# A decoder layer on one core: the state-space loop's end-of-chunk scaling, moved from VectorE to ScalarE

## The chip, the cores and the metric

The kernel runs on one core of a Trainium2 chip. The metric is the device time of one execution, in microseconds (us). A core has TensorE (matrix products, into PSUM), VectorE, ScalarE, GpSimd (called POOL in the profile) and SyncE (SP), whose queue issues the DMAs. Each engine works through its own instructions in order, and they wait for one another by semaphores.

## The reference, cut to what matters

The layer takes 1024 tokens of width 128 and a context of 6404 rows. It runs a bidirectional state-space block (mamba2), then cross attention to the context with 8 heads, then a mixture of 8 experts. The change lies in the state-space block, which the reference computes for each direction (forward on one half of the width, backward on the other) as a scan over the tokens:

```python
dA = jnp.exp(dt * A)
dtx = dt[..., None] * xh

def step(h, inp):
    dA_t, dtx_t, B_t, C_t = inp
    h = dA_t[:, :, None, None] * h + jnp.einsum('bhp,bn->bhpn', dtx_t, B_t)
    return (h, jnp.einsum('bhpn,bn->bhp', h, C_t))
...
y = jnp.moveaxis(ys, 0, 1) + xh * D[None, None, :, None]
y = y.reshape(b, l, D_INNER) * jax.nn.silu(z)
y = _rmsnorm(y, gnorm_w)
return y @ outp_w.T
```

There are 2 heads of 64 in a direction, and the state has 128 rows.

## The kernel before

The scan is computed in `TC` = 8 chunks of 128 tokens, both directions (`q` = 0, 1) side by side, so that most tiles are 128 x 256: two directions of two heads of 64 columns. Chunk c needs, in this order:

- **`decay_rows`** and **`turned_rows`** (TensorE, for chunk c + 1 inside chunk c): rows of decays into the bank `DECAY`, and the convolved inputs `xc` and `Bc` transposed into the bank `TURNED_XB`.
- **`decays`** (VectorE, L1391): four scans that make the decay matrix `LT`. **`mixing`** (VectorE, L1417): `LT` times the product of B and C (`gram`) gives `Mt`.
- **`inputs`** (VectorE): L1405 makes `Xp`, the inputs times their step dt; L1409 makes `Xw`, that is `Xp` times the decay from each token to the chunk's end, `dcy[:, 1]`. Both are one instruction of 128 x 256. The last chunk needs no `Xw`.
- **`state_rows`** (ScalarE, L989): copies the transposed B out of PSUM as `Bm`.
- In `chunk_pe` (TensorE): the product of C with the old state `Hp` (`ys_ps`); then, behind the waits for `bm_done` and `xw_done`, the product of `Bm` and `Xw` (`s_ps`), which is what the chunk adds to the state; then `turn_gate` of the chunk before, `decay_rows` and `turned_rows` of the next; then the inside product of `Mt` and `Xp` (`yi_ps`); then, in the first `BESIDE` = 4 chunks, two convolutions of the second half of the tokens with `project_out` of the chunk before and `gram` of the next between them.
- **`chunk_act`** (ScalarE): four scaled copies (L1009) of the product with the old state into `t1`; `gate_turned` (L995); `state_rows` of the next chunk; the silu of the first convolution; in some chunks a cast of the context (`high_ctx`, L982); `gate_out` (L1001); the silu of the second convolution (L973 or L976); then, behind `yg_done`, two squares with a sum (L1035) of the gated output.
- **`state`** (VectorE, L1428): four instructions update `Hp`. **`gated`** (VectorE, L1441 and L1444): `t1` plus the inside product, times silu(z), gives `yg`.

VectorE's order in a chunk is `mixing`, `state`, `decays` of the next chunk, `gated`, `inputs` of the next chunk, and then a piece of other work: in chunk 0 the means, variances and inverse roots of the first half of the context, in chunks 1 and 2 statistics of the second half (L1332), in chunk 3 its aggregation (L1357) and roots, and small pieces later. The roots release GpSimd, which scales the context rows. The order on every engine is written out by hand. The convolutions of the second half share PSUM bank 7, so each waits for the silu of the one before:

```python
if n == 7:
    pe.wait_ge(silu_done, 1)
elif n == 8:
    pe.wait_ge(silu_done, 7)
elif n > 8:
    pe.wait_ge(silu_done, n)
```

`Bm` and `Xw` lie in two buffers each, taken in turn by c % 2, in `m_arena`; `Xp`, `t1`, `yg` and `Hp` lie in `w_arena`. When the last chunk's `yg` is there, SP starts the transposing DMAs of the context, and VectorE adds the block's outputs to the residual (L1513), norms the rows and so prepares the queries. Then TensorE finds the row maxima and runs the attention, which takes most of the time, and the experts.

Of the kernel before, what the change touches and what calls it, by code (L numbers as in the profile page):

```python
# [21 lines left out]
ACT, ALU, AX = mybir.ActivationFunctionType, mybir.AluOpType, mybir.AxisListType  # L22
# [4 lines left out]
TC = T // P  # L27
# [3 lines left out]
HD = 64  # L31
# [187 lines left out]
def layer(nc, a, out):  # L219
    ctx = ExitStack()  # L220
    with ctx:  # L221
# [97 lines left out]
        Xp = take([2, 2, P])  # L319
# [16 lines left out]
        dtc, dcy = take([6, 2, TC, 2]), take([3, 2, TC, 2])  # L336
# [13 lines left out]
        Bm, Xw = take([2, 2, P]), take([2, 2, P])  # L350
# [61 lines left out]
        da_ps, xb_ps, g_ps, s_ps, ys_ps, yi_ps = (sem(n) for n in ("da_ps", "xb_ps", "g_ps", "s_ps", "ys_ps", "yi_ps"))  # L412
        gt_ps, gt_sb, out_ps, out_evac = (sem(n) for n in ("gt_ps", "gt_sb", "out_ps", "out_evac"))
        lt_done, xp_done, xw_done, m_done, h_done = (sem(n) for n in ("lt_done", "xp_done", "xw_done", "m_done", "h_done"))
# [510 lines left out]
        def _(act):  # L925
            s = nc.scalar
# [31 lines left out]
            for q in range(2):  # L958
                s.activation(Wout[:, q], PS[:, 7, (1 + q) * P:(2 + q) * P], ACT.Copy,
                             scale=V["gw_" + "fb"[q]]).then_inc(op_sb, 1)  # L960
# [6 lines left out]
            def silu_conv(n):  # L967

                (q, r), half = CONV[n % 8], n // 8
                act.wait_ge(conv_ps, n + 1)  # L970
                if r < 3:
                    dst, bias = (xc, Bc, Cc)[r][:, q, half * QB:(half + 1) * QB], cbias[:, q, r:r + 1]
                    s.activation(dst, PS[:, conv_bank(n), :], ACT.Silu, bias=bias, scale=1 / (XS * WS)).then_inc(silu_done, 1)  # L973
                else:
                    dst = (zs_f, zs_b)[q][:, 4 * half:4 * half + 4, :].rearrange("p c n -> p (c n)")
                    s.activation(dst, PS[:, conv_bank(n), :], ACT.Silu, scale=1 / (XS * WS)).then_inc(silu_done, 1)  # L976
# [7 lines left out]
            def state_rows(c):  # L984
# [3 lines left out]
                    act.wait_ge(s_ps, c - 1)  # L988
                s.copy(Bm[:, c % 2], halves_of(TURNED_XB, 1)).then_inc(bm_done, 1)  # L989

            def gate_turned(c):

                act.wait_ge(gt_ps, c + 1)
                after(act, out_ps, c)
                s.copy(ygT, halves_of(GATE)).then_inc(gt_sb, 1)  # L995
# [7 lines left out]
            def chunk_act(c):  # L1003

                act.wait_ge(ys_ps, c + 1)
                after(act, y2_done, c)
                for q in range(2):
                    for h in range(2):
                        last = s.activation(t1[:, q, h * HD:(h + 1) * HD],  # L1009
                                            PS[:, FROM_STATE, q * P + h * HD:q * P + (h + 1) * HD], ACT.Copy,  # L1010
                                            scale=dcy[:, 0, q, c, h:h + 1])
                last.then_inc(t1_done, 1)
                if c:
                    gate_turned(c - 1)
                if c + 2 < TC:
                    state_rows(c + 1)
                if c < BESIDE:
                    silu_conv(8 + 2 * c)
                if c == TC - 1:
                    root(2)  # L1020
                if 2 <= c < NSOON - 1:
                    high_ctx(c - 2)
                elif c == NSOON - 1:
                    s.activation(rt[:, 5, 0:1], iota8[:, 0:1], ACT.Sqrt)
                elif c == NSOON:
                    high_ctx(c - 3)
                if c:
                    gate_out(c - 1)
                if c < BESIDE:
                    silu_conv(9 + 2 * c)  # L1030
                act.wait_ge(yg_done, c + 1)
                for q in range(2):
                    if c or q:
                        act.wait_ge(sq_done, 2 * c + q)
                    s.activation(sq, yg[:, c % 2, q], ACT.Square, accum_out=ssy[:, q, c:c + 1]).then_inc(sq_done, 1)  # L1035

            for n in range(6):
                silu_conv(n)
            state_rows(0)
            for n in range(6, 8):  # L1040
                silu_conv(n)
            for c in range(TC):
                chunk_act(c)
            gate_turned(TC - 1)
# [212 lines left out]
        def _(dve):  # L1257
            v = nc.vector
# [29 lines left out]
            for c in range(TC):  # L1288
                last = v.bn_stats(stx[:, c, :], x_sb[:, c, :])
# [105 lines left out]
            def inputs(c):  # L1395

                dve.wait_ge(xb_ps, c + 1)
                if c + 1 < TC:
                    dve.wait_ge(bm_done, c + 1)
                if c >= 2:  # L1400
                    dve.wait_ge(yi_ps, c - 1)
                    dve.wait_ge(s_ps, c - 1)
                by_head = lambda x: x.rearrange("p q (h d) -> p q h d", h=2)
                wide = lambda x: x.unsqueeze(3).to_broadcast([P, 2, 2, HD])
                v.tensor_tensor(by_head(Xp[:, c % 2]), by_head(halves_of(TURNED_XB)), wide(dtc[:, 3, :, c, :]),  # L1405
                                ALU.mult).then_inc(xp_done, 1)
                dve.wait_ge(xp_done, c + 1)
                if c + 1 < TC:
                    v.tensor_tensor(by_head(Xw[:, c % 2]), by_head(Xp[:, c % 2]), wide(dcy[:, 1, :, c, :]),  # L1409
                                    ALU.mult).then_inc(xw_done, 1)  # L1410

            def mixing(c):

# [1389 lines left out]
```

## Time and profile before

| | |
|---|---|
| median of 3 runs | 1702.06 us (1701.68 to 1702.9) |
| the profiled execution's own time | 1701.74 us |
| its span in the profile | 1699.7 us |
| mean granted TensorE clock | 0.993 of full speed |
| TensorE busy | 1655.4 us, 97% |
| VectorE busy | 1323.0 us, 78% |
| ScalarE busy | 1069.0 us, 63% |
| GpSimd busy | 873.6 us, 51% |

The times of the views count from the start of the span. Busy time is that of the instructions alone. A row of the timeline gives the start, the time from the start of its first instruction to the end of its last, the engine, the line of the kernel, the operation, what is written from what, and in brackets how long the engine was idle ahead of it and which engine's work ended that. PE is TensorE, DVE VectorE, ACT ScalarE, SPq the queue of SP. The timeline puts like instructions that follow one another in one row ("x4"); next ones may start before the last one's end, as they are pipelined.

### The profile page before, as it was taken

To read this page: it belongs to the slowest core of one execution; us is meant where nothing else is said; L and a number is where in the kernel's file an instruction comes from. 1 tells how busy PE (TensorE), PEld (TensorE's weight loads), DVE (VectorE), ACT (ScalarE), POOL (GpSimd) and SP (SyncE) were. 2 spreads that over 40 slices of the span, in tenths; PEclk is the share of its full clock that TensorE was granted. 3 is DMA by queue.
4 is the path that set the end of the run, shared out by engine and by line. 5 is a ranking of instruction groups with operands and counts; after the bars stand their busy time and mean duration, and the time that the engine had idled before them with its cause. 6 is when DMAs were issued, how large, how long until landed. Compare 5 with 4: busy or idle time off the path is not lost. (4 is left out here: it accounts for less than half of the span.)

```text
span 1699.7 us, 31706 instructions
## 1 busy us (share of the span) xinstructions
PE 1655.4 (97%) x9115; PEld 846.5 (50%) x9115; DVE 1323.0 (78%) x2315; ACT 1069.0 (63%) x1310; POOL 873.6 (51%) x723
## 2 busy tenths in 40 slices
PE   6889999999999999999999999999999999999997
PEld 5754444444444444445454444445454545444496
DVE  7988989877777777777777777777777777776687
ACT  5545665666666666666566666666666666667674
POOL 4767992055454545454545545454545454452365
PEclk9989999999999999999999999999999999999998
DMA  5032110000000000000000000000000000000262
GB/s 186 2 61 73 56 42 0 1 1 1 1 0 0 0 0 0 0 0 0 0 0 1 0 1 0 1 0 1 0 0 0 1 0 1 1 0 1 77 213 77
DMA packets 41058, 34.06 MB, mean 20 GB/s; under 512 B 20447, under 2 KB 35299, under 8 KB 40598
## 3 DMA queue, kind: packets, MB, share of 16 engines
q1 hardware_dynamic: 39862, 30.70, 6.2%
q0 software_dynamic: 1120, 2.31, 0.4%
q8 instruction: 52, 0.85, 0.2%
q14 instruction: 24, 0.20, 0.0%
HBM read 15.27 MB, written 4.23 MB: 11 GB/s over the span
## 5 line engine op out<-in xcount | busy, mean ns | idle before, releaser
L851 POOL TENSOR_TENSOR p_arena<-p_arena 128x512 f16<-128x512 f32 x364 | 596.3, 1638 | 670.8 <-ACT p_arena L1131 670.8
L1122 ACT ACTIVATE p_arena<-PS 128x1024 f16<-128x1024 f32 (+1 forms) x480 | 484.8, 1010 | 508.0 <-PE PS L2032 508.0
L2032 PE MATMUL PS<-a_arena,z_arena 128*128 128x512 f16 (+1 forms) x2832 | 746.5, 380 | 1.4 <-DVE a_arena L1894 1.4
L1578 DVE TENSOR_REDUCE mxs<-PS 128x512 f32 (+1 forms) x900 | 599.7, 672 | 184.5 <-PE PS L2032 180.1
L2032 PE MATMUL PS<-p_arena,z_arena 128*128 128x512 f16 x2800 | 740.2, 379 | 0.4 <-ACT p_arena L1140 0.4
L1131 ACT ACTIVATE p_arena<-PS 128x1024 f32<-128x1024 f32 (+1 forms) x480 | 481.6, 1003 | 0.0
L1610 DVE TENSOR_TENSOR p_arena<-p_arena 128x512 f16<-128x512 f32 (+1 forms) x480 | 395.5, 824 | 85.9 <-ACT p_arena L1131 79.9
L2032 PEld LDWEIGHTS PS<-a_arena,z_arena 128*128 (+1 forms) x2832 | 274.4, 98 | 325.6 <-issue 1.9
L2032 PEld LDWEIGHTS PS<-p_arena,z_arena 128*128 128x128 f16 (+1 forms) x2800 | 271.6, 98 | 313.3 <-ACT p_arena L1140 0.9
L2032 PE MATMUL PS<-z_arena,a_arena 128*128 (+3 forms) x1024 | 352.7, 359 | 3.6 <-DVE mxs L1578 1.9
L2032 PEld LDWEIGHTS PS<-z_arena,a_arena 128*128 128x128 f16 (+1 forms) x1024 | 97.7, 98 | 126.2 <-issue 6.2
L844 POOL TENSOR_TENSOR w_arena<-w_arena 128x256 f16<-128x256 f32 (+1 forms) x50 | 42.1, 842 | 4.2
L781 POOL TENSOR_SCALAR p_arena<-p_arena,mv,rs 128x127 f32<-128x127 f32 x50 | 41.8, 853 | 0.0
L840 POOL TENSOR_SCALAR w_arena<-w_arena 128x256 f32<-128x256 f32 (+1 forms) x50 | 41.4, 828 | 0.0
L2032 PE MATMUL PS<-w_arena 128*128 128x512 f16 (+5 forms) x268 | 35.7, 271 | 3.0 <-DVE w_arena L1326 2.6
L906 POOL TENSOR_TENSOR p_arena<-z_arena,p_arena 128x512 f16<-128x512 f32 x22 | 25.6, 1162 | 25.0 <-ACT p_arena L1217 24.7
L1879 DVE TENSOR_REDUCE mxs<-PS 128x2 f32<-128x1024 f32 (+1 forms) x30 | 33.6, 1184 | 3.4 <-PE PS L2032 3.0
L1608 DVE TENSOR_TENSOR p_arena<-p_arena 4x512 f16<-4x512 f32 x16 | 10.9, 682 | 31.8 <-ACT p_arena L1131 31.8
L2032 PEld LDWEIGHTS PS<-VO,p_arena 128*128 128x128 f32 x256 | 33.4, 191 | 4.3
L897 POOL DMA_INDIRECT xg_dram<-ah_arena,r_arena x14 | 15.0, 1070 | 37.8 <-DVE ah_arena L1751 33.9
L2032 PE MATMUL PS<-z_arena,w_arena 128*128 128x128 f16 x504 | 33.3, 219 | 0.8 <-DVE z_arena L1923 0.3
L2032 PE MATMUL PS<-VO,p_arena 128*128 128x130 f32 (+1 forms) x256 | 33.7, 275 | 0.0
(339 smaller groups left out, 984.7 us busy)
## 6 DMA issues: line engine op xcount, KB each, us to landing
w_arena<-w_arena SPq DMA_DIRECT2D x26, 256.0 KB
w_arena<-in_L_ffn_gate_up_w SPq DMA_DIRECT2D x8, 512.0 KB
p_arena<-w_arena SPq DMA_DIRECT2D x26, 128.0 KB
p_arena<-in_ctx SPq DMA_DIRECT2D x2, 1600.0 KB
w_arena<-in_L_ffn_down_w SPq DMA_DIRECT2D x8, 256.0 KB
a_arena<-in_L_xattn_Wkv SPq DMA_DIRECT2D x1, 1024.0 KB, 7.1
a_arena<-xg_dram SPq DMA_DIRECT2D x12, 65.0 KB, 2.1
xg_dram<-VO SPq DMA_DIRECT2D x1, 715.0 KB, 7.1
```

Source lines behind the costliest of these rows:

```text
L781: g.tensor_scalar(ctx_sb[:, c, 1:P], ctx_sb[:, c, 1:P], mv[:, c, 0:1], rs[:, 3, c:c + 1], ALU.subtract, ALU.mult).then_inc(z_scaled, 1)
L840: g.tensor_scalar(src, src, WS, 0.0, ALU.mult, ALU.add).then_inc(w_scaled, 1)
L844: g.tensor_tensor(lo, src, hi, ALU.subtract).then_inc(stage_used, 1)
L851: g.tensor_tensor(Plo[:, r % 3, QB:2 * QB], P32[:, r % 2, QB:2 * QB], Phi[:, r % 3, QB:2 * QB], ALU.subtract).then_inc(pl_ready, 1)
L897: g.indirect_dma_start(xg_dram, bass.IndirectOffsetOnAxis(ap=posu[:, k, t:t + 1], axis=0), xrow_f[:, k, t, :], None).then_inc(sent, 16)
L906: g.tensor_tensor(lo, hid[:, u % RING], hi, ALU.subtract).then_inc(f_lo, 1)
L1122: s.activation(Phi[:, r % 3, 0:w], ps, ACT.Exp, scale=1 / SSC).then_inc(hi_ready, 1)
L1131: s.activation(P32[:, r % 2, 0:w], ps, ACT.Exp, scale=1 / SSC).then_inc(p32_ready, 1)
L1578: v.tensor_reduce(mxs[:, i, bass.ds(kb, 1)], PS[:, 6 + par, 0:w], AX.X, ALU.max).then_inc(mx_read, 1)
L1610: v.tensor_tensor(Plo[:, r % 3, at:w], P32[:, r % 2, at:w], Phi[:, r % 3, at:w], ALU.subtract).then_inc(lo_ready, 1)
L1879: v.tensor_reduce(mxs[:, i:i + 2, kb:kb + 1], PS[:, pair % 2 * 2:pair % 2 * 2 + 2, 0:w], AX.X, ALU.max).then_inc(mx_read, 2)
L2032: return t.matmul(o, l, r, start=start, stop=stop)
```

## The change

VectorE no longer makes `Xw`: L1409 and the wait ahead of it go. In its place ScalarE gets a function `state_inputs(c)` with four scaled copies of 128 x 64, one for each direction and head, because the scale of an activation is one column. `state_inputs(0)` stands behind the last silu of the first half and ahead of the first chunk; `state_inputs(c + 1)`, for chunks 1 to 6, stands at the end of `chunk_act(c)`, behind the two squares. TensorE still waits for `xw_done` ahead of the state product, and `Xw` keeps its two buffers.

```diff
@@ -988,6 +988,17 @@
                     act.wait_ge(s_ps, c - 1)
                 s.copy(Bm[:, c % 2], halves_of(TURNED_XB, 1)).then_inc(bm_done, 1)
 
+            def state_inputs(c):
+
+                act.wait_ge(xp_done, c + 1)
+                if c >= 2:
+                    act.wait_ge(s_ps, c - 1)
+                for q in range(2):
+                    for h in range(2):
+                        cols = slice(h * HD, (h + 1) * HD)
+                        last = s.activation(Xw[:, c % 2, q, cols], Xp[:, c % 2, q, cols], ACT.Copy, scale=dcy[:, 1, q, c, h:h + 1])
+                last.then_inc(xw_done, 1)
+
             def gate_turned(c):
 
                 act.wait_ge(gt_ps, c + 1)
@@ -1033,12 +1044,15 @@
                     if c or q:
                         act.wait_ge(sq_done, 2 * c + q)
                     s.activation(sq, yg[:, c % 2, q], ACT.Square, accum_out=ssy[:, q, c:c + 1]).then_inc(sq_done, 1)
+                if c + 2 < TC:
+                    state_inputs(c + 1)
 
             for n in range(6):
                 silu_conv(n)
             state_rows(0)
             for n in range(6, 8):
                 silu_conv(n)
+            state_inputs(0)
             for c in range(TC):
                 chunk_act(c)
             gate_turned(TC - 1)
@@ -1404,10 +1418,6 @@
                 wide = lambda x: x.unsqueeze(3).to_broadcast([P, 2, 2, HD])
                 v.tensor_tensor(by_head(Xp[:, c % 2]), by_head(halves_of(TURNED_XB)), wide(dtc[:, 3, :, c, :]),
                                 ALU.mult).then_inc(xp_done, 1)
-                dve.wait_ge(xp_done, c + 1)
-                if c + 1 < TC:
-                    v.tensor_tensor(by_head(Xw[:, c % 2]), by_head(Xp[:, c % 2]), wide(dcy[:, 1, :, c, :]),
-                                    ALU.mult).then_inc(xw_done, 1)
 
             def mixing(c):
 
```

ScalarE's order from the silu of the second convolution of chunk 1 to the first instructions of chunk 2, before (`m_arena` holds `Bm` and `Xw`, and `ssy` the sums of the squares):

```order
L973 ACTIVATE z_arena<-PS,vecs 128x512 [waits conv_ps]
L1035 ACTIVATE w_arena,ssy<-w_arena 128x128 [waits sq_done,yg_done]
L1035 ACTIVATE w_arena,ssy<-w_arena 128x128 [waits sq_done]
L1009 ACTIVATE w_arena<-PS,wt_arena 128x64 [waits y2_done,ys_ps]
L1009 ACTIVATE w_arena<-PS,wt_arena 128x64 x3
L995 COPY w_arena<-PS 128x256 [waits out_ps,gt_ps]
```

and the same place with the change (its lines are numbered 11 higher from `gate_turned` on, and L1046 and L1020 are the squares and the copies into `t1`):

```order
L973 ACTIVATE z_arena<-PS,vecs 128x512 [waits conv_ps]
L1046 ACTIVATE w_arena,ssy<-w_arena 128x128 [waits sq_done,yg_done]
L1046 ACTIVATE w_arena,ssy<-w_arena 128x128 [waits sq_done]
L999 ACTIVATE m_arena<-w_arena,wt_arena 128x64 [waits s_ps,xp_done]
L999 ACTIVATE m_arena<-w_arena,wt_arena 128x64 x3
L1020 ACTIVATE w_arena<-PS,wt_arena 128x64 [waits y2_done,ys_ps]
```

The four copies L999 now stand between the squares of one chunk and `t1` of the next, behind the silu L973.

VectorE's order from the gated output of chunk 3 to the aggregation of the context's second half, before:

```order
L1441 TENSOR_TENSOR w_arena<-w_arena,PS 128x256 [waits gt_ps,sq_done,t1_done,yi_ps]
L1444 TENSOR_TENSOR w_arena<-w_arena,z_arena 128x128 [waits y2_done]
L1444 TENSOR_TENSOR w_arena<-w_arena,a_arena 128x128
L1405 TENSOR_TENSOR w_arena<-PS,wt_arena 128x256 [waits yi_ps,s_ps,bm_done,xb_ps]
L1409 TENSOR_TENSOR m_arena<-w_arena,wt_arena 128x256 [waits xp_done]
L1357 BN_AGGR mv<-st 128x2 x25
```

and with the change (L1451, L1454, L1419 and L1371 are the same statements):

```order
L1451 TENSOR_TENSOR w_arena<-w_arena,PS 128x256 [waits gt_ps,sq_done,t1_done,yi_ps]
L1454 TENSOR_TENSOR w_arena<-w_arena,z_arena 128x128 [waits y2_done]
L1454 TENSOR_TENSOR w_arena<-w_arena,a_arena 128x128
L1419 TENSOR_TENSOR w_arena<-PS,wt_arena 128x256 [waits yi_ps,s_ps,bm_done,xb_ps]
L1371 BN_AGGR mv<-st 128x2 x25
```

The product into `m_arena` and its wait are gone, and the aggregation follows `Xp` at once.

## Rows read from the trace of the kernel before

**Rows 1.** The page, part 1: busy us, share of the span, instructions.
```profile
PE 1655.4 (97%) x9115; PEld 846.5 (50%) x9115; DVE 1323.0 (78%) x2315; ACT 1069.0 (63%) x1310; POOL 873.6 (51%) x723
```

**Rows 2.** Timeline of ScalarE, 36 to 88 us: last silu, squares, copies.
```profile
37.36 0.60 ACT L976 ACTIVATE a_arena<-PS 128x512 f32<-128x512 f32 x1 [0.35 <-PE PS L2032]
...
45.19 0.30 ACT L1035 ACTIVATE w_arena<-w_arena 128x128 f32<-128x128 f32 x1
...
45.92 0.91 ACT L1009 ACTIVATE w_arena<-PS,wt_arena 128x64 f32<-128x64 f32 x4
...
53.79 0.30 ACT L1035 ACTIVATE w_arena<-w_arena 128x128 f32<-128x128 f32 x1
...
61.29 0.30 ACT L1035 ACTIVATE w_arena<-w_arena 128x128 f32<-128x128 f32 x1
...
68.83 0.30 ACT L1035 ACTIVATE w_arena<-w_arena 128x128 f32<-128x128 f32 x1
...
75.90 0.31 ACT L1035 ACTIVATE w_arena<-w_arena 128x128 f32<-128x128 f32 x1 [0.40 <-DVE w_arena L1444]
...
87.15 0.31 ACT L1035 ACTIVATE w_arena<-w_arena 128x128 f32<-128x128 f32 x1 [0.21 <-DVE w_arena L1444]
```

**Rows 3.** Timeline of TensorE: state products (from m_arena) and three inside products.
```profile
37.80 0.61 PE L2032 MATMUL PS<-m_arena 128*128 128x128 f32 x4
...
44.85 0.61 PE L2032 MATMUL PS<-m_arena 128*128 128x128 f32 x4
...
48.07 0.49 PE L2032 MATMUL PS<-w_arena,z_arena 128*128 128x128 f32 x2 [0.83 <-DVE w_arena L1417]
...
53.45 0.61 PE L2032 MATMUL PS<-m_arena 128*128 128x128 f32 x4
...
55.67 0.39 PE L2032 MATMUL PS<-w_arena,z_arena 128*128 128x128 f32 x2
...
61.99 0.61 PE L2032 MATMUL PS<-m_arena 128*128 128x128 f32 x4
...
69.54 0.61 PE L2032 MATMUL PS<-m_arena 128*128 128x128 f32 x4
...
73.03 0.49 PE L2032 MATMUL PS<-w_arena,z_arena 128*128 128x128 f32 x2 [1.11 <-DVE w_arena L1417]
...
76.80 0.68 PE L2032 MATMUL PS<-m_arena 128*128 128x128 f32 x4 [0.82 <-DVE m_arena L1409]
...
82.51 0.68 PE L2032 MATMUL PS<-m_arena 128*128 128x128 f32 x4 [0.56 <-DVE m_arena L1409]
```

**Rows 4.** Timeline of VectorE: the removed product, what follows it, a late mixing.
```profile
67.13 0.42 DVE L1409 TENSOR_TENSOR m_arena<-w_arena,wt_arena 128x256 f32<-128x256 f32 x1
...
67.47 1.75 DVE L1357 BATCH_NORM_AGGREGATE mv<-st 128x2 f32<-128x6 f32 x25
...
72.29 0.69 DVE L1417 TENSOR_TENSOR w_arena<-w_arena,PS 128x512 f32<-128x512 f32 x1
```

**Rows 5.** Behind the loop: SP's first transposes, granted clock, TensorE products at either clock.
```profile
91.93 10.98 SPq L642 DMA_TRANSPOSE z_arena<-z_arena  x3
...
core 0: us, PE busy (x) PEld busy (x) DVE busy (x) ACT busy (x) POOL busy (x), PEclk, DMA share, GB/s
88.00:90.00 2.00, 0.79 (x7) 0.69 (x7) 1.81 (x10) 1.21 (x6) 2.00 (x4) 1.00 0.00 0
...
96.00:97.00 1.00, 1.00 (x4) 0.60 (x3) 0.90 (x7) 0.42 (x1) 0.00 (x0) 0.50 1.16 217
...
95.21 1.22 PE L2032 MATMUL PS<-Tm,a_arena 128*128 128x256 f32 x2
...
101.45 0.70 PE L2032 MATMUL PS<-Tm,a_arena 128*128 128x256 f32 x2
```

**Rows 6.** Timeline of ScalarE ahead of the loop: scaled copies of other sizes.
```profile
11.05 1.71 ACT L936 ACTIVATE ah_arena<-w_arena,wt_arena 128x256 f32<-128x256 f32 x4 [1.72 <-DVE wt_arena L1298]
...
13.13 0.69 ACT L941 ACTIVATE w_arena<-PS,nw 128x512 f16<-128x512 f32 x1 [0.37 <-DVE nw L1305]
...
13.72 0.47 ACT L942 ACTIVATE w_arena<-PS,nw 128x256 f16<-128x256 f32 x1
```

## The prediction

> **What bounds the kernel now.** I read the page first. TensorE is busy for 97% of the span and VectorE for 78% [rows 1], so the kernel as a whole follows TensorE. The change, though, touches only the state-space loop, which fills about 38 to 92 us, and there an average over the whole span says nothing. Below, s(c) is TensorE's product of Bm and Xw for chunk c, y(c) its inside product (Mt and Xp), sq(c) the first of ScalarE's two squares of that chunk.
>
> I then read the timeline, engine by engine, for who waits for whom at s(c). Before, s(c) runs at 37.80, 44.85, 53.45, 61.99, 69.54, 76.80 and 82.51 us [rows 3]. ScalarE starts the squares of the chunk before at 45.19, 53.79, 61.29, 68.83 and 75.90 us [rows 2]. So in the chunks with convolutions TensorE is at s(c) at about the time when ScalarE only begins the squares of the chunk before: 44.85 against 45.19, 53.45 against 53.79, 61.99 against 61.29, 69.54 against 68.83. The squares come late because they stand behind the silu of the second convolution of the chunk. VectorE had written Xw long before. This order is the whole case: the copies are moved from an engine that was early to a place behind the squares.
>
> VectorE is the limit twice: y(1) at 48.07 and y(4) at 73.03 both waited for its mixing L1417 [rows 3], held up by the statistics of the context. The rest of the kernel hangs on the end of the loop: the first transposing DMA starts at 91.93 us, when the last gated chunk is there [rows 5].
>
> **What is removed.** Seven VectorE products L1409 of 0.42 us. The next operation starts 0.34 us after such a product starts (67.13 to 67.47) [rows 4], so 0.34 us a chunk is what VectorE gets back, 2.4 us in all. It reaches the end only where VectorE is what is waited for.
>
> **What is added.** Seven blocks of four ScalarE copies of 64 columns, from SBUF, scaled by a column. No row shows just this. Nearest are the four scaled copies L1009 of 64 columns out of PSUM, 0.91 us [rows 2], and the four scaled copies L936 of 256 columns out of SBUF, 1.71 us [rows 6]. Columns cost (0.69 - 0.47) / 256 = 0.86 ns each by L941 and L942 [rows 6], so 192 fewer in each of four take 0.66 us off 1.71. I take this 1.05 us, as it keeps the SBUF source and the column scale; 0.9 and 1.7 us are the outer bounds. By the same rate the 256 columns take 0.22 us of the 1.05 and the four starts 0.83, 0.21 each; a single copy would be 0.43 us, and six of those in the chain would make the sum 3.7 us less, but the scale differs by direction and head and is one column, so it takes four. The Trainium skill (VectorE: DVE Perf Modes, on the errata of SBUF sources) says that SBUF's latency is paid once per instruction and advises tiles of 512 elements or more; the trace's 0.21 us a start agrees, and by that rule the change loses more on ScalarE than it takes off VectorE.
>
> From the start of a chunk's squares to ScalarE's next instruction it is 45.92 - 45.19 = 0.73 us [rows 2]. A wait passes to TensorE in about 0.05 us (mixing ends at 72.98, y(4) starts at 73.03) [rows 3, 4]. So s(c+1) can start no earlier than sq(c) + 0.73 + 1.05 + 0.05, rounded to **sq(c) + 1.85 us**.
>
> **Chunk by chunk** (times as before plus the shift so far):
> - s(0): the copies start when the last silu L976 ends, 37.36 + 0.60 = 37.96 [rows 2]; s(0) is then at 39.06 instead of 37.80: +1.3. TensorE's decay and turned rows stand behind s(0), and all of chunk 0 moves by that.
> - s(1): 45.19 + 1.3 + 1.85 = 48.3 instead of 44.85: +3.5. But y(1) had waited for VectorE until 48.07. From s to y it is 55.67 - 53.45 = 2.2 us where nothing waits [rows 3]. So y(1) is at 50.5: +2.5. A us of the delay goes into TensorE's old idle time.
> - s(2): 53.79 + 2.5 + 1.85 = 58.1: +4.7.
> - s(3): 61.29 + 4.7 + 1.85 = 67.8: +5.9.
> - s(4): 68.83 + 5.9 + 1.85 = 76.6: +7.0. The mixing of chunk 4, at 72.29 before [rows 4], moves by 5.9 less the 0.34 saved ahead of it: +5.5. So y(4) could start at 73.03 + 5.5 = 78.5 for VectorE and at 76.6 + 2.2 = 78.8 for TensorE; before, VectorE's decays stood between y(4) and the squares, and I let these follow VectorE: sq(4) = 75.90 + 5.5 = 81.4.
> - s(5): 81.4 + 1.85 = 83.3 instead of 76.80: +6.5.
> - s(6): from s to the same chunk's squares it is 87.15 - 82.51 = 4.6 us [rows 2, 3], so the loop's own circle is now 4.6 + 1.85 = 6.5 us; s(6) = 89.8 instead of 82.51: +7.3.
> - The last chunk has no Xw and keeps its length. The loop ends **7.3 us** later.
>
> What stands behind moves with it. On ScalarE, t1 of the same chunk now waits behind the copies, but VectorE needs it only behind y(c), over 3 us later. GpSimd's second half of scaling starts with VectorE's statistics, +5.5 us, and stays ahead of its readers. SP's transposes stand behind the end of the loop; nothing is moved past them. I cost all these at nothing beyond the 7.3 us.
>
> The profiled execution took 1701.74 us for a span of 1699.7 us, and becomes 1709.0; the median of the runs, 1702.06, is 0.3 us above it, so the forecast for the median is **1709.4 us**, 0.43% slower. Differences under 0.2%, 3.4 us, count as no change.
>
> **The rivals.**
> 1. *VectorE is what the loop waits for, and the copies slip into ScalarE's idle time.* Each chunk then gets VectorE's 0.34 us back, seven of them 2.4 us: 1702.06 - 2.4 = 1699.7 us, not slower, and inside 0.2%; only if still more came back would it be faster. It decides if Xw is ready before TensorE reaches s(c), that is if sq(c) starts at least 1.85 us ahead of s(c+1). The rows give a head start of -0.3, -0.3, 0.7, 0.7 and 0.9 us. None is enough: 4%, half of it for a kernel faster by over 0.2%. The Trainium skill (Perfetto Trace Analysis, on optimizing Scalar and DVE operations) says that work may be handed to ScalarE where VectorE is saturated; VectorE is busy for most of this loop, and by that rule this rival would be the forecast.
> 2. *The delay is absorbed.* If half of it were, by work behind the loop that doesn't depend on the loop's end, the time would be about 1705.5 us, the edge of no change. For it: TensorE has idle time after 93 us. Against: that idle time waits for VectorE and ScalarE, whose work there starts from the loop's end, and 91.93 us is the start of a chain of transposes. 5%.
> 3. *TensorE's clock falls inside the loop.* The granted clock was 1.00 from 88 to 90 us, with TensorE busy for 0.79 of 2 us, and had fallen to 0.50, that is 1.2 GHz, by 96 to 97 us [rows 5]. Two products of 256 columns took 1.22 us at that level and 0.70 us at 2.4 GHz [rows 5]. The new waits of some 2 us before s(c) thin out TensorE's work. At the lower level the 2.2 us of TensorE's work from s(c) to y(c) would take 1.22 / 0.70 = 1.74 times as long, 1.6 us more a chunk; over three chunks 4.9 us: 1714.3 us. Against: over a whole chunk TensorE stays busy for well over half. 8%.
>
> **How the numbers follow.** The forecast's own mechanism gets 83%. Its unknown is the block: at 0.9 us instead of 1.05, six blocks in the chain give 0.9 us back (1708.5); at 1.2 us they cost 0.9 more (1710.3); at 1.7 us, 1713.3. The handing over from ScalarE and the start of the attention add perhaps 1 or 2 us either way. The range 1705.5 to 1713.5 leaves out most of rivals 1 and 3 and part of 2. The forecast and rival 3 make slower 0.91; rival 2 and half of rival 1 make no change 0.07; the other half is faster, 0.02.
>
> **What would show it.** On ScalarE, four copies of about 1.05 us behind each pair of squares; TensorE idle before s(1) to s(6), put down to these copies, for 1 to 2.5 us each; s(c) at about 39.1, 48.3, 58.1, 67.8, 76.6, 83.3 and 89.8 us; the first transpose at about 99.2 us. The start of the attention, its length and the expert stage should be unchanged but for that shift. I am wrong if the squares start earlier than now and leave room for the copies; if the first transpose is late by 7 us but the span is not; or if the granted clock is under 1.00 between 38 and 90 us.

## The result, and the profile after

| | before | changed |
|---|---|---|
| median (beside each other, 4 runs each) | 1702.48 us | 1712.12 us |
| the profiled execution's own time | 1701.74 us | 1710.77 us |
| its span | 1699.7 us | 1708.7 us |
| first transposing DMA, the end of the loop | 91.93 us | 100.89 us |

The ratio is 1.0054, with a 95% interval of 1.0043 to 1.0066: the kernel became about 9 us slower. The forecast was 1709.4 us and slower, with a range of 1705.5 to 1713.5. One of the 23 executions of the kernel before that stand beside e5 to e8 below was a slow one of 4650.54 us, and it is in no ratio.

The page of the changed kernel, part 1, answers to [rows 1]:

```profile
PE 1654.9 (97%) x9115; PEld 847.2 (50%) x9115; DVE 1316.7 (77%) x2308; ACT 1075.4 (63%) x1338; POOL 872.6 (51%) x723
```

VectorE has 7 instructions and 6.3 us less, ScalarE 28 instructions and 6.4 us more, TensorE the same work. By busy time this looks like a fair trade. The 9 us do not show here at all.

They show in TensorE's timeline, at the state products s(0) to s(6) [rows 3]. The rows of the changed kernel, with the idle time ahead of each and what ended it:

```profile
38.72 0.68 PE L2042 MATMUL PS<-m_arena 128*128 128x128 f32 x4 [1.08 <-ACT m_arena L999]
...
48.11 0.68 PE L2042 MATMUL PS<-m_arena 128*128 128x128 f32 x4 [2.10 <-ACT m_arena L999]
57.94 0.68 PE L2042 MATMUL PS<-m_arena 128*128 128x128 f32 x4 [2.10 <-ACT m_arena L999]
...
67.78 0.68 PE L2042 MATMUL PS<-m_arena 128*128 128x128 f32 x4 [1.05 <-ACT m_arena L999]
...
76.62 0.92 PE L2042 MATMUL PS<-m_arena 128*128 128x128 f32 x4 [1.06 <-ACT m_arena L999]
84.98 0.68 PE L2042 MATMUL PS<-m_arena 128*128 128x128 f32 x4 [1.59 <-ACT m_arena L999]
91.89 0.68 PE L2042 MATMUL PS<-m_arena 128*128 128x128 f32 x4 [1.77 <-ACT m_arena L999]
```

All seven now wait for the new copies, L999, and 10.8 us of TensorE's idle time is put down to them. The forecast had 39.1, 48.3, 58.1, 67.8, 76.6, 83.3 and 89.8 us: right to within 0.4 us as far as s(4), then 1.7 and 2.1 us too early. This trace was already 0.33 us early ahead of the loop (the last silu at 37.03 instead of 37.36); counted from that silu, the forecast is right to within 0.4 us as far as s(4), then 2.0 and 2.4 us too early.

ScalarE's timeline around one of these waits (chunk 0 to chunk 1; compare [rows 2]) shows the chain link by link:

```profile
45.60 0.69 ACT L973 ACTIVATE z_arena<-PS,vecs 128x512 f32<-128x512 f32 x1 [1.56 <-PE PS L2042]
46.19 0.30 ACT L1046 ACTIVATE w_arena<-w_arena 128x128 f32<-128x128 f32 x1
46.38 0.19 ACT L1046 ACTIVATION_READ_ACCUMULATOR w_arena<-w_arena 128x1 f32 x1
46.61 0.31 ACT L1046 ACTIVATE w_arena<-w_arena 128x128 f32<-128x128 f32 x1
46.82 0.19 ACT L1046 ACTIVATION_READ_ACCUMULATOR w_arena<-w_arena 128x1 f32 x1
46.92 1.05 ACT L999 ACTIVATE m_arena<-w_arena,wt_arena 128x64 f32<-128x64 f32 x4
```

Silu, squares with their two reads of the sum, then the copies: 1.05 us, just what the estimate had. They end at 47.97 and TensorE starts at 48.11, a hand-over of 0.14 us where I had 0.05. ScalarE had been idle for 1.56 us ahead of that silu, and that is where the copies would have fitted (e8 and e10 put them into such a place).

What the sum did not have is chunk 4. The stretches of the changed kernel (columns as in [rows 5]; the granted clock is the third number from the end), and three rows of TensorE's timeline, the third of them a chunk later:

```profile
74.00:75.00 1.00, 0.31 (x4) 0.15 (x2) 0.90 (x11) 0.83 (x4) 0.00 (x0) 1.00 0.00 0
75.00:76.00 1.00, 0.56 (x4) 0.37 (x4) 0.86 (x6) 0.97 (x6) 0.00 (x0) 1.00 0.00 0
76.00:77.00 1.00, 0.38 (x3) 0.41 (x4) 0.85 (x5) 1.00 (x6) 0.00 (x0) 0.96 0.00 0
77.00:78.00 1.00, 1.00 (x7) 1.00 (x7) 0.91 (x4) 0.27 (x2) 0.29 (x3) 0.50 0.00 0
...
79.00:80.00 1.00, 1.00 (x7) 1.00 (x6) 0.03 (x1) 0.00 (x0) 1.00 (x2) 0.50 0.00 0
80.00:81.00 1.00, 1.00 (x10) 1.00 (x9) 0.87 (x3) 0.25 (x1) 1.00 (x2) 0.83 0.00 0
...
83.00:84.00 1.00, 0.39 (x4) 0.20 (x2) 1.00 (x3) 0.93 (x5) 1.00 (x2) 1.00 0.00 0
84.00:85.00 1.00, 0.02 (x1) 0.05 (x1) 1.00 (x2) 1.00 (x6) 1.00 (x1) 1.00 0.00 0
```

```profile
78.18 1.92 PE L2042 MATMUL PS<-I,wt_arena 128*128 128x128 f32 x8
...
80.55 0.39 PE L2042 MATMUL PS<-w_arena,z_arena 128*128 128x128 f32 x2
...
85.94 1.06 PE L2042 MATMUL PS<-I,wt_arena 128*128 128x128 f32 x8
```

From 77 to a little past 80 us TensorE ran at 1.2 GHz; in the 3 us ahead of that it had been busy for 1.25 us. It was thinly busy again from 83 to 85 us, for 0.41 of 2 us, and the clock stayed at 1.00. The eight passes of the decay rows took 1.92 us at the low clock and 1.06 us a chunk later, and from s(4) to y(4) it was 80.55 - 76.62 = 3.9 us, where the chunk before took 2.3.

### The profile page after: what moved, and what is told of

The parts are those of the page before. It is cut to its first block and busy times, and to the rows that moved or that the text cites. A ratio compares the mean times of both kernels' runs of the same rounds, so it can differ in the third digit from the quotient of the medians.

```text
span 1708.7 us, 31731 instructions
## 1 busy us (share of the span) xinstructions
PE 1654.9 (97%) x9115; PEld 847.2 (50%) x9115; DVE 1316.7 (77%) x2308; ACT 1075.4 (63%) x1338; POOL 872.6 (51%) x723
## 5 line engine op out<-in xcount | busy, mean ns | idle before, releaser
L840 POOL TENSOR_SCALAR w_arena<-w_arena 128x256 f32<-128x256 f32 (+1 forms) x50 | 34.7, 695 | 0.0
```

The costliest lines, as they stand in the source:

```text
L840: g.tensor_scalar(src, src, WS, 0.0, ALU.mult, ALU.add).then_inc(w_scaled, 1)
```

## The experiments

The traces of different executions start a few tenths of a us, up to two us, apart ahead of the loop. So I count from the start of the last silu ahead of it (L976 into `a_arena`, 37.36 us before and 37.03 us after). Every number is the start in that execution's timeline less that start.

| run | s(0) | s(1) | s(2) | s(3) | s(4) | s(5) | s(6) | first transpose |
|---|---|---|---|---|---|---|---|---|
| before | 0.44 | 7.49 | 16.09 | 24.63 | 32.18 | 39.44 | 45.15 | 54.57 |
| changed | 1.69 | 11.08 | 20.91 | 30.75 | 39.59 | 47.95 | 54.86 | 63.86 |
| e1 wait alone | 0.44 | 8.80 | 17.68 | 26.56 | 34.44 | 41.40 | 47.15 | 56.56 |
| e2 work alone | 0.44 | 7.50 | 16.09 | 24.63 | 32.18 | 39.42 | 45.14 | 54.58 |
| e3 chunk 0 alone | 1.69 | 8.81 | 17.41 | 25.95 | 33.49 | 40.75 | 46.45 | 55.87 |
| e4 one copy | 1.14 | 9.97 | 19.25 | 28.53 | 36.81 | 43.32 | 49.46 | 58.60 |
| e5 changed again | 1.69 | 11.08 | 20.91 | 30.75 | 39.58 | 47.92 | 54.83 | 63.83 |
| e6 kept busy | 1.69 | 11.08 | 20.92 | 30.75 | 39.59 | 46.30 | 53.22 | 62.46 |
| e7 ahead of squares | 1.69 | 10.35 | 19.45 | 28.57 | 36.67 | 43.51 | 49.84 | 59.22 |
| e8 early copies, early mixing | 0.44 | 7.49 | 14.99 | 23.54 | 31.13 | 38.06 | 43.77 | 53.20 |
| e9 early mixing alone | 0.44 | 7.49 | 14.99 | 24.05 | 31.60 | 38.75 | 46.06 | 55.49 |
| e10 early copies alone | 0.44 | 7.49 | 15.74 | 24.28 | 31.82 | 38.74 | 44.44 | 53.85 |
| e11 e8 with filled idle time behind | 0.44 | 7.49 | 14.99 | 23.54 | 31.11 | 38.03 | 43.73 | 53.15 |
| e12 before with the same filling | 0.44 | 7.49 | 16.08 | 24.63 | 32.17 | 39.40 | 45.13 | 54.56 |

The columns repeat to a few hundredths wherever nothing differs (changed and e5, before and e2), so a tenth of a us can be read from them. The times of whole executions can't give that: the kernel before alone went from 1705.2 to 1708.8 us over 31 runs on one chip. Its median was 1702.48 us beside the changed kernel, but 1706.66 us beside e1 to e4, 1705.72 beside e5 to e8 and 1705.94 beside e9 to e12. The absolute times in the expectations start from the 1702 us of the first, so below every run is compared by its ratio to the kernel before beside it.

The theory: a chain silu, squares, copies, s(c+1) now closes each chunk, and its length is the sum of its links; the granted clock adds a piece in chunk 4. The rivals: that ScalarE's load costs, whoever waits; that the wait alone costs; that the hand-over between engines costs and not the length.

### e1: the wait without the work

```diff
                     pe.wait_ge(xw_done, c + 1)
+                    after(pe, sq_done, 2 * c)
```

> The kernel before, in which VectorE still makes Xw, but TensorE's state product of chunk c also waits for ScalarE's two squares of chunk c - 1. This is the changed kernel's place in the order without its copies. Theory (the place behind the squares and the length of the copies add up in one chain): s(c+1) at sq(c) + 0.73 + 0.05, that is about 46.0, 54.7, 63.3, 70.9, 78.0 and 83.7 us, and the first transpose at about 93.1 us, 1.2 us later than before; time about 1703.5. Rival, that the place alone is what costs, because TensorE then waits for work behind a silu: most of the 9 us, 1708 or more. Rival, that only ScalarE's extra work costs: nothing, first transpose at 91.9.

Measured: first transpose 2.0 us later than before, ratio 1.001 (1.000 to 1.0019). TensorE's row at s(1):

```profile
46.60 0.68 PE L2032 MATMUL PS<-m_arena 128*128 128x128 f32 x4 [1.15 <-ACT w_arena L1035]
```

The place behind the squares costs 2.0 us by itself, not the bulk. I had 1.2: s(c+1) came 0.97 us behind sq(c) and not 0.78, because the last read of the sum ends 0.82 us behind the start of the squares and the hand-over, from the end of the work on ScalarE to the start on TensorE, takes 0.15.

### e2: the work without the wait

```diff
+            def spare_copies(c):
+
+                act.wait_ge(xp_done, c + 1)
+                for q in range(2):
+                    for h in range(2):
+                        cols = slice(h * HD, (h + 1) * HD)
+                        s.activation(acc[:, q, cols], Xp[:, c % 2, q, cols], ACT.Copy, scale=dcy[:, 1, q, c, h:h + 1])
...
                     s.activation(sq, yg[:, c % 2, q], ACT.Square, accum_out=ssy[:, q, c:c + 1]).then_inc(sq_done, 1)
+                if c + 2 < TC:
+                    spare_copies(c + 1)
```

> The kernel before, with VectorE making Xw, and on ScalarE the four copies of chunks 1 to 6 all the same behind the squares, into a spare tile that nobody reads. ScalarE's load is that of the change without anyone waiting for it. Theory: t1 and what follows on ScalarE come up to 1 us later and nobody needs them by then; first transpose at 91.9 to 92.3 us, time within 0.5 us of before. Rival, that ScalarE's load itself lengthens the loop: first transpose 5 us or more later, near 98.

Measured: 54.58 against 54.57 us, ratio 1.0002 (0.9992 to 1.0011). Six microseconds of extra work on ScalarE, in the very place, cost nothing when nobody waited for it. This ends the rival of ScalarE's load, and it shows what "ScalarE is busy for 63%" is worth: nothing, for or against.

### e3: chunk 0 alone

```diff
-                if c + 2 < TC:
-                    state_inputs(c + 1)
...
+                dve.wait_ge(xp_done, c + 1)
+                if 0 < c < TC - 1:
+                    v.tensor_tensor(by_head(Xw[:, c % 2]), by_head(Xp[:, c % 2]), wide(dcy[:, 1, :, c, :]),
+                                    ALU.mult).then_inc(xw_done, 1)
```

(Against the changed kernel.)

> The changed kernel with only the copies of chunk 0 on ScalarE, ahead of the loop; for chunks 1 to 6 VectorE makes Xw as before. Theory: s(0) 0.9 to 1.3 us later than 37.80, of which VectorE gives 0.34 back before chunk 1's mixing: y(1) and all behind it about 0.6 us later, first transpose at 92.5 us, time about 1702.9. Rival, that this first delay is what the whole loss grows from (each chunk adding to it): 4 us or more.

Measured: s(0) 1.25 us later and the first transpose 1.30 us later; ratio 1.0005 (0.9996 to 1.0015). So the first delay doesn't grow, but nothing of it came back either. My 0.34 was wrong here: what VectorE saves ahead of chunk 0's mixing it spends waiting for s(0) in `state`, ahead of which it was idle for 2.01 us (0.35 before). A saving ahead of an engine's own wait is no saving.

### e4: one copy instead of four

```diff
-                for q in range(2):
-                    for h in range(2):
-                        cols = slice(h * HD, (h + 1) * HD)
-                        last = s.activation(Xw[:, c % 2, q, cols], Xp[:, c % 2, q, cols], ACT.Copy, scale=dcy[:, 1, q, c, h:h + 1])
-                last.then_inc(xw_done, 1)
+                s.activation(Xw[:, c % 2], Xp[:, c % 2], ACT.Copy, scale=dcy[:, 1, 0, c, 0:1]).then_inc(xw_done, 1)
```

> The changed kernel with one ScalarE copy of 256 columns with one scale in place of the four of 64 with their own. It leaves out the separate scales of the two heads and directions. Theory: the block takes about 0.45 us instead of 1.05, s(c+1) at sq(c) + 1.23; worked through as in the prediction s = 38.1, 46.7, 55.9, 65.0, 73.0, 79.9 and 86.1 us, first transpose 3.5 us later than before, at about 95.5, TensorE's clock at 1.00 until then, time about 1705.7. Rival, that what counts is the handing over between engines and not the length of the block: 1709 or more, as in the changed kernel.

Measured: first transpose 4.0 us later than before (3.5 expected), ratio 1.0017 (1.0008 to 1.0027). That is 2.0 us over the wait alone, 0.7 of it at s(0). The one copy took 0.49 us against 1.05 for the four. The length of the block goes into the chain, and the three extra starts of instructions are worth nearly 4 us of the change's loss (58.60 here, 62.46 in e6 with the clock held), close to the 3.7 us of the prediction. The granted clock was 1.00 from 74 to 92 us.

### e5 and e6: TensorE's clock in chunk 4

e5 is the changed kernel unaltered; e6 adds to it

```diff
+                    if c:
+                        pe.wait_ge(lt_done, c + 1)
+                        for _ in range((0, 9, 9, 4, 4, 6, 7)[c]):
+                            mm(PS[:, DECAY, :], I16[:], xTh[:, 0, 0:QB])
                     pe.wait_ge(bm_done, c + 1)
                     pe.wait_ge(xw_done, c + 1)
```

> The changed kernel unaltered, beside the next three on one chip. Times here are from the start of the last silu ahead of the loop, 37.36 us in the trace before and 37.03 in the one after; the first transpose was then at 54.57 before and at 63.86 after. Theory: the loop's end is made of the chain through the copies (7.6 us) and of TensorE's clock at 1.2 GHz in chunk 4 (1.7 us). If that fall comes with the idle time that the change makes, it comes again: first transpose at 63.9, granted clock under 1.00 between 74 and 92 us. If it was a chance of that one execution, the first transpose is at 62.2 and the clock 1.00 there.

> The changed kernel, with products of 128 x 512 in half precision that nobody reads put into TensorE's idle time ahead of the state products of chunks 1 to 6 (9, 9, 4, 4, 6 and 7 of them, some 0.22 us each, into the bank of the decay rows, which is free then). Theory: granted clock 1.00 through the loop, chunk 4 from s(4) to s(5) back from 8.36 to about 6.7 us, first transpose at 62.2 us from the last silu in place of 63.86, time 1.7 us under the changed kernel's beside it. Rival, that chunk 4 was long for another reason (VectorE's roots, or reads of PSUM in each other's way): 63.9 all the same.

Measured: e5 repeated the changed kernel in every column to 0.03 us, with the clock at 0.50 in chunk 4 again. In e6 it stayed at 1.00; s(4) to s(5) took 6.71 us instead of 8.34, and the loop ended 1.4 us earlier. The stretch of chunk 4 and its row of decay rows in e6:

```profile
79.00:81.00 2.00, 2.00 (x20) 2.00 (x20) 1.90 (x9) 0.77 (x3) 1.18 (x4) 1.00 0.03 8
```

```profile
79.70 1.06 PE L2042 MATMUL PS<-I,wt_arena 128*128 128x128 f32 x8
```

So the clock's fall is a consequence of the new idle time, not chance, and it costs 1.6 us in chunk 4, of which 1.4 are left at the loop's end. The ratios to the kernel before were 1.0060 (1.0042 to 1.0078) for e5 and 1.0032 (1.0021 to 1.0043) for e6. That is 4.1 us between the two medians, more than the loop's 1.4. Another 1.0 us lies behind the loop: the last reduction of the first block's row maxima (`mcol` in the expectations below) started 2.4 us earlier in e6 (115.14 against 117.58 us from the last silu). The rest I can't place: e5 had only four runs.

### e7: the copies ahead of the squares

```diff
+                if c + 2 < TC:
+                    state_inputs(c + 1)
                 act.wait_ge(yg_done, c + 1)
                 for q in range(2):
                     if c or q:
                         act.wait_ge(sq_done, 2 * c + q)
                     s.activation(sq, yg[:, c % 2, q], ACT.Square, accum_out=ssy[:, q, c:c + 1]).then_inc(sq_done, 1)
-                if c + 2 < TC:
-                    state_inputs(c + 1)
```

> The changed kernel with the four copies ahead of the two squares instead of behind them; everything else as changed. Theory: each s(c+1) comes 0.7 us earlier in the convolution chunks; from the last silu s = 1.7, 10.3, 19.3, 28.3, 36.3, 43.4 and 49.8 us, first transpose at 59.2 us, 4.6 us later than before and 4.7 earlier than as changed. Rival, that the silu of the second convolution is what holds the copies and the squares add nothing: s(4) at 39.6 and the transpose at 62 or later.

Measured: 59.22 us, as expected, ratio 1.0028 (1.0018 to 1.0038), and the clock at 1.00 through the loop. Two statements exchanged give half of the loss back, 4.6 of 9.3 us; 1.4 of it is the clock, which did not fall, and 3.2 is the order (62.46 in e6). What is left is the silu ahead of the copies of chunks 1 to 4. In the last two the copies waited 0.74 and 0.47 us for VectorE's `Xp` (L1419), and there 1.05 us stands on the path in place of VectorE's 0.42.

### e8 to e10: where ScalarE had been idle

ScalarE makes Xw of chunks 1, 2 and 4 only, early (e10); VectorE's mixing of chunks 1 and 4 stands ahead of the roots of the context (e9); both (e8). Against the kernel before, with `state_inputs` as in the change:

```diff
+        BY_ACT = (1, 2, 4)
...
                 if c < BESIDE:
                     silu_conv(8 + 2 * c)
+                if c + 1 in BY_ACT:
+                    state_inputs(c + 1)
...
-                if 2 <= c < NSOON - 1:
+                if 2 <= c < NSOON - 1 and c != 3:
...
                     silu_conv(9 + 2 * c)
+                if c == 3:
+                    high_ctx(c - 2)
...
                 dve.wait_ge(xp_done, c + 1)
-                if c + 1 < TC:
+                if c + 1 < TC and c not in BY_ACT:
```

```diff
             for c in range(TC):
-                mixing(c)
+                if c not in (1, 4):
+                    mixing(c)
...
                     ctx_aggr(0, CC // 2)
+                    mixing(1)
...
                     settle(v.bn_aggr(mv[0:LEFT, CC, :], st6[0:LEFT, CC, :]))
+                    mixing(4)
```

> An attempt at better than both: ScalarE makes Xw only for chunks 1, 2 and 4, right behind the silu of the first convolution, where it sat idle for 1.3 us or more (in chunk 3 with the context cast moved behind the second silu); VectorE makes the others; and VectorE's mixing of chunks 1 and 4 stands behind the aggregation of the context's statistics and ahead of its roots, where TensorE waited 1.1 and 1.4 us for it. Theory: y(1) 1.0 us earlier than before and y(4) 2.3, of which VectorE's roots leave 1.3; first transpose at 53.2 us from the last silu, 1.3 earlier than before, time 1.3 us (0.08%) under the kernel before. Rival, that VectorE's total work in chunks 0 to 2 sets the pace: first transpose at 54.2 or later.

> The kernel before with only the second part of the last attempt: VectorE's mixing of chunks 1 and 4 ahead of the roots of the context, and all of Xw on VectorE. Counted from the last silu: y(1) 1.0 us earlier, but VectorE reaches mixing(2) no earlier than before, which leaves 0.6 of that; y(4) earlier, VectorE's roots then hold the decays. Theory: first transpose at 53.9, 0.7 us earlier than before; ScalarE's early copies brought the other 0.7 of 1.4. Rival, that the reordering did all of it: 53.2. Rival, that it did nothing: 54.6.

> The kernel before with only the first part: ScalarE makes Xw of chunks 1, 2 and 4 right behind the silu of the first convolution, VectorE the others, no reordering of mixing. Theory: the move to ScalarE is worth the 0.34 us that VectorE gets back wherever VectorE is waited for, before y(1) and before y(4), where there are two of them: first transpose at 53.9, 0.7 us earlier than before, so that the same move which cost 9 us behind the squares gains where ScalarE was idle. Rival, that no placing on ScalarE can gain because four copies take 1.05 us and one product 0.42: 54.6 or later.

Measured at the first transpose: e10 0.7 us earlier than before (ratio 0.9996, 0.9987 to 1.0005), e8 1.4 us earlier (0.9994, 0.9984 to 1.0003). Both loops came out as expected, and the whole times can't be told from before. ScalarE's timeline in e8, for the place that was empty:

```profile
42.43 0.69 ACT L974 ACTIVATE z_arena<-PS,vecs 128x512 f32<-128x512 f32 x1 [2.21 <-PE PS L2051]
43.01 1.05 ACT L1000 ACTIVATE m_arena<-w_arena,wt_arena 128x64 f32<-128x64 f32 x4
44.68 0.69 ACT L974 ACTIVATE z_arena<-PS,vecs 128x512 f32<-128x512 f32 x1 [0.61 <-PE PS L2051]
```

The same four copies, 1.05 us long, and ScalarE still waits 0.61 us for TensorE behind them.

e9 went the other way: first transpose at 55.49, 0.9 us later than before, ratio 1.000 (0.9991 to 1.0009). Up to s(5) it was ahead by 0.7 us; then s(5) to s(6) took 7.31 us instead of 5.71. The expectation had 53.9 and none of this. TensorE's rows there, and the granted clock:

```profile
78.23 0.68 PE L2035 MATMUL PS<-m_arena 128*128 128x128 f32 x4 [2.09 <-DVE m_arena L1409]
...
79.20 1.63 PE L2035 MATMUL PS<-I,wt_arena 128*128 128x128 f32 x8
```

```profile
76.00:77.00 1.00, 0.14 (x2) 0.00 (x0) 0.97 (x4) 0.00 (x0) 1.00 (x3) 1.00 0.00 0
77.00:78.00 1.00, 0.00 (x0) 0.00 (x0) 0.97 (x4) 0.65 (x4) 1.00 (x2) 1.00 0.00 0
...
80.00:81.00 1.00, 1.00 (x6) 1.00 (x6) 0.72 (x5) 0.00 (x0) 1.00 (x2) 0.50 0.00 0
```

With y(4) early, TensorE was done with chunk 4 sooner and then waited 2.09 us for VectorE; the clock fell to 1.2 GHz, the decay rows took 1.63 us instead of 1.06, and the chunk lost more than the reordering had brought. No run holds the clock in e9, so that all of the 1.6 us is the clock's is argued and not shown. In e8 TensorE waited 1.86 us at the same place and the clock stayed at 1.00; whether the 0.23 us made the difference isn't shown either.

In e8, of the 1.4 us gained in the loop, only 0.1 was left at the last reduction of the first block's row maxima (107.60 against 107.74). Behind the loop TensorE runs out of work, and its transposes of the queries then ran slowly (first row: the idle time; second: eight transposes; then the clock):

```profile
101.53 0.17 PE L2051 MATMUL PS<-I,z_arena 4*128 4x4 f16 x1 [3.42 <-ACT z_arena L1111]
102.54 2.14 PE L2290 MATMUL PS<-I,m_arena 128*128 128x128 f32 x8 [0.84 <-DVE m_arena L1559]
105.11 2.72 PE L2051 MATMUL PS<-z_arena,ah_arena 128*128 128x512 f16 x6 [0.43 <-issue]
```

```profile
103.00:105.00 2.00, 1.68 (x8) 0.97 (x6) 1.20 (x4) 0.87 (x2) 1.04 (x1) 0.50 0.08 16
```

### e11 and e12: the clock behind the loop

e11 is e8 with, e12 the kernel before with

```diff
                 if kind == "left":
+                    for _ in range(13):
+                        mm(PS[:, 3, :], I16[:], xTh[:, 0, 0:QB])
                     pe.wait_ge(z_hi, N_HI)
```

> The attempt with early copies and early mixing, and 13 products of 128 x 512 in half precision that nobody reads in TensorE's idle time behind the loop, ahead of the transposes of the queries. In the attempt itself the loop ended 1.4 us earlier but the first row maxima came 0.1 us earlier only, with the granted clock at 0.50 from 104 to 108 us and the eight transposes at 2.14 us in all. Theory: TensorE's clock stays at 1.00 there, the transposes take about 1.2 us of work and the six products behind them 1.5 instead of 2.7; the end of the first block's row maxima (mcol) at 105.5 to 106.5 us from the last silu instead of 107.6, and the time 2 to 3 us (0.15%) under the kernel before. Rival, that the stretch is bound by VectorE and ScalarE and not by the clock: mcol at 107.5, time as the attempt's.

> The kernel before with the same 13 products behind the loop and nothing else. Theory: the clock there was low from 94 to 101 us in the kernel before and up again by 102, where it mattered for the transposes; the six products behind them ran at the low clock. mcol 0.5 to 1.2 us earlier than 107.74, time up to 1 us under before. Rival: the products only delay what stands behind them, up to 1 us slower.

Measured: e11 1703.95 us against 1705.94, ratio 0.9989 (0.9980 to 0.9998), by 2 us, the one version whose interval lies under the kernel before. It does so by a hair, and with twelve versions tried one such interval can be chance. e12: 1.0002 (0.9993 to 1.0011), no gain. The transposes in e11:

```profile
104.99 0.66 PE L2290 MATMUL PS<-I,m_arena 128*128 128x128 f32 x4 [0.84 <-DVE m_arena L1559]
106.01 0.65 PE L2290 MATMUL PS<-I,m_arena 128*128 128x128 f32 x4 [0.36 <-DVE m_arena L1559]
107.09 2.42 PE L2051 MATMUL PS<-z_arena,ah_arena 128*128 128x512 f16 x6 [0.43 <-issue]
```

The transposes ran at the full clock, as expected, but the six products behind them took 2.42 us, with the clock down again from 107.4 us, and the last reduction of the row maxima started at 107.14 us, 0.6 earlier than before and not the 1.2 to 2.2 that I had expected. Of e11's 2 us I can show only this 0.6.

In e12 the 13 products, the transposes and the six products behind them, and the clock over the first two:

```profile
102.30 2.98 PE L2032 MATMUL PS<-w_arena,I 128*128 128x512 f16 x13
...
105.31 1.09 PE L2271 MATMUL PS<-I,m_arena 128*128 128x128 f32 x8
107.42 1.46 PE L2032 MATMUL PS<-z_arena,ah_arena 128*128 128x512 f16 x6 [1.01 <-ACT z_arena L1078]
```

```profile
102.00:104.00 2.00, 2.00 (x11) 0.89 (x10) 1.93 (x9) 0.71 (x3) 0.12 (x1) 1.00 0.55 106
104.00:106.00 2.00, 2.00 (x13) 1.17 (x12) 0.60 (x3) 0.17 (x1) 1.04 (x1) 1.00 0.14 29
```

The clock was back at 1.00 before the 13 products began, as in the kernel before, and it then stayed there, where in the kernel before it fell again between 104 and 106 us. The six products took 1.46 us instead of 2.62. But the 13 took 2.98 us, in a place where TensorE had been idle for 0.65, 0.44 and 0.36 us, so the six products started 1.7 us later than before (counted from the last silu), and the last reduction of the row maxima started at 108.24, 0.5 us late. The rival held: the products delayed what stands behind them, by more than the clock gave back. In e11 the same 13 products also took 2.98 us, but in e8 TensorE had stood idle for 3.42 us there. Filling in work helps as far as it fits into the idle time.

## Why the prediction was right or wrong

- **Who waits for whom at s(c).** Right. The comparison of [rows 2] with [rows 3], TensorE at s(c) when ScalarE only begins the squares, was the case: all seven waits are put down to L999, and e2 shows that without the wait the work is free. Two sentences beside it read [rows 3] too narrowly: TensorE had waited 0.82 and 0.56 us for L1409 itself at s(5) and s(6), so VectorE had not written Xw long before in the last chunks, and it was the limit at more than two places. The sum doesn't use this, as it goes by the squares.
- **The price of the block, 1.05 us.** Right to the hundredth. The four copies took 0.33 us each, overlapping. The row with the same source and the same kind of scale, L936 less its extra columns, was the one to take; the nearer-looking L1009 (0.91 us) would have been 0.14 short.
- **sq(c) + 1.85.** Short by 0.07: 1.92 us, at s(1) (48.11 - 46.19). ScalarE's end to TensorE's start takes 0.14 us, where I had taken 0.05 from VectorE.
- **The shift by chunk.** Forecast +1.3, +3.5, +4.7, +5.9, +7.0, measured +1.25, +3.59, +4.82, +6.12, +7.41. That y(1) would swallow one us of the delay was right (50.41 us, +2.67 from the last silu).
- **The last chunks.** Forecast +6.5 and +7.3, measured with the clock held (e6) +6.86 and +8.07. The circle s(5) to s(6) is 6.9 us, not 6.5. I had taken the 4.6 us from s to the squares out of chunk 6, which turns two tiles of inputs fewer than chunk 5, as the last chunk needs no B; in chunk 5 it was 4.80 before (81.60 - 76.80) and 4.97 changed (52.92 - 47.95 from the last silu). The 0.17 between these two stays open.
- **The clock.** Rival 3, at 8%, came true, in one chunk. Its step "over a whole chunk TensorE stays busy for well over half" was the wrong test: the clock fell after a few us of thin work on both sides of a chunk's border. Priced at 1.6 us a chunk, it cost 1.6 in chunk 4. The prediction had named a clock under 1.00 between 38 and 90 us as a sign of being wrong, and on this point it was: the forecast's own mechanism put the clock at nothing.
- **The sum.** 7.3 us forecast; at the loop's end 9.3 measured: 2.0 for the wait alone (e1), 2.0 for one copy in it (e4), 3.9 for making it four (e6 less e4), 1.4 for the clock (changed less e6). Without the clock 7.9. The median moved by 9.6 us, to 1712.12, inside the range. That is luck in part: the room above 1709.4 was put there for a dearer block and for the handing over, the block cost what was forecast, and the room was taken up by the clock and the last chunks.
- **What stands behind.** t1, GpSimd's scaling and the transposes were rightly costed at nothing. From the first transpose to the last reduction of the first block's row maxima it took 53.7 us after and 53.2 before.
- **Rival 1.** It lacked the place. Behind the squares the move cost 9 us; at the idle places of chunks 0, 1 and 3 it gained 0.7 us in the loop (e10), too little to show in the whole time. The Trainium skill (Perfetto Trace Analysis, on optimizing Scalar and DVE operations) says that handing work to ScalarE may make sense where VectorE is saturated.

## What to carry to other kernels

Before moving work to a less busy engine, find the moment when its consumer waits for it and ask what the new engine will be doing just then; put it into the idle time that precedes, not behind the last thing in the loop's body. The price of such a move is the whole length of the new producer from its last release to its last instruction, starts of small instructions included, while the engine that is relieved gives back something only where it is itself waited for. And waits of one or two us on TensorE can cost as much again through the clock, in the chunk that follows, though most of them here did not.

## What the runs showed of the hardware that I had not expected

- TensorE's granted clock fell to 0.50 inside a loop in which it is busy for most of the time: after 1.06 us of idle time close behind 0.69 us in the changed kernel, after 2.09 us in e9. The same waits of 2.10 us ahead of s(1) and s(2) left it at 1.00, so the length of one wait doesn't tell. Nor does the busy time of 2 us around it: 0.41 us from 83 to 85 us in the changed kernel left it up. What decides is open. It happened at the same place in both profiled executions of the changed kernel.
- Products that nobody reads held the clock (e6 and e12) or delayed its fall (e11). Where they were longer than the idle time they stood in, they cost more than the clock gave back: 2.98 us of them saved 1.16 us on the six products and the row maxima came half a us late (e12).
- A scaled copy of 64 columns out of SBUF takes 0.33 us, and four in a row 1.05 us, against 0.90 us for four out of PSUM in the same trace.
- The squares' sums cost a read of 0.19 us each on ScalarE, and the last one lies in the chain where TensorE waits for the squares (e1: 0.82 us from the start of the first square to the end of the last read). The four copies of the changed kernel start before that read has ended, 0.73 us behind the first square.
